# Every fourth stored o unit copied out of PSUM by VectorE instead of ScalarE

## The reference, cut to what matters

```python
# layer 0: four Gaussian kernels over adj (8, 1024, 1024)
w  = exp(-0.5 * (adj[..., None] - mean)**2 / (1e-14 + precision**2))
w  = w / sum(w, axis=-1)                     # over the four kernels
ws = sum(w, axis=2)                          # row sums, (8, 1024, 4)
x  = layernorm(x + concat_k(ws[..., k] * (x @ W_k.T)))
# layer 1: one of four experts for each batch, picked by argmax
W   = expert_w[argmax(mean_rows(x) @ router_w + router_b)]
out = adj @ (x @ W)
y   = relu(batchnorm over all rows of the same expert (out))
x   = layernorm(x + y)
```

## Time and profile before

| what | before |
|---|---|
| time, median of 3 runs | 892.62 us (890.96 to 893.26) |
| time of the profiled execution | 888.44 us |
| its span | 886.7 us |
| busy PE | 751.8 us, 85% |
| busy DVE | 754.0 us, 85% |
| busy ACT | 766.9 us, 86% |
| busy POOL | 687.5 us, 78% |

### The profile page before, as it was taken

The page is one execution under the profiler, slowest core; times in us unless marked ns, Lnnn a source line. Parts: engine busy times, 40 slices in busy tenths (PEclk is TensorE's granted clock), DMA queues, the critical chain, the costliest instruction groups (busy, mean ns, idle before and its releaser), DMA issues.

```text
span 886.7 us, 12501 instructions
## 1 busy us (share of the span) xinstructions
PE 751.8 (85%) x3922; PEld 349.1 (39%) x3922; DVE 754.0 (85%) x1639; ACT 766.9 (86%) x774; POOL 687.5 (78%) x773
## 2 busy tenths in 40 slices
PE   1444469899999999999999999999999989996671
PEld 1111124344444444444444444444444434444440
DVE  1999988899999999999999999999999981226994
ACT  5999998999999999999999999999999941116983
POOL 6699999999988888888888888888888441004794
PEclk9966679999999999999999999999999999998996
DMA  8799886898897779777977797789786636219999
GB/s 229 200 282 257 189 243 166 221 202 206 201 240 192 192 190 240 196 194 190 237 198 191 195 240 196 192 189 242 198 190 161 124 141 263 95 64 396 356 383 366
DMA packets 263925, 191.71 MB, mean 216 GB/s; under 512 B 210098, under 2 KB 210098, under 8 KB 262322
## 3 DMA queue, kind: packets, MB, share of 16 engines
q1 hardware_dynamic: 263714, 190.90, 79.3%
q10 hardware_dynamic: 144, 0.00, 0.0%
HBM read 91.78 MB, written 48.76 MB: 159 GB/s over the span
## 4 chain that ended last, share of the span: by engine, by line
ACT 38%; DVE 27%; POOL 19%; PE 9%; issue 4%; DMA 1%; SPq 0%; POOLq 0%; DVEq 0%; ACTq 0%
DVE ps_t L953 19%; ACT wgt L647 13%; ACT ps_t L656 6%; ACT ps_t L658 6%; ACT adj_in L641 5%; ACT ps_t L652 5%; PE ps_z L1118 5%; POOL adj_cut L505 3%; DVE x_in L937 3%; DVE wgt L915 3%; PE ps_o L1136 2%; POOL adj_in L500 2%; POOL x_turn L516 2%; PE ps_t L1136 2%; POOL adj_cut L503 2%
## 5 line engine op out<-in xcount | busy, mean ns | idle before, releaser
L1118 PE MATMUL ps_z<-adjT,x1p 128*128 128x512 f16 x1536 | 341.7, 379 | 0.5 <-POOL x1p L542 0.5
L953 DVE TENSOR_TENSOR ps_t<-ps_t,wgt 128x1024 f32<-128x1024 f32 x192 | 234.8, 1223 | 28.0 <-ACT ps_t L652 26.9
L1104 PE MATMUL ps_h<-w0T,x_turn 128*128 128x512 f16 x768 | 194.5, 407 | 75.1 <-DVE x_in L937 64.2
L915 DVE SCALAR_TENSOR_TENSOR wgt<-wgt,ps_t 128x1024 f32<-128x1024 f32 x192 | 224.7, 1214 | 15.8 <-ACT ps_t L658 15.8
L1118 PEld LDWEIGHTS ps_z<-adjT,x1p 128*128 128x128 f16 x1536 | 150.0, 98 | 181.3 <-POOL x1p L542 1.0
L641 ACT ACTIVATE wgt<-adj_in,neg_mu 128x1024 f32<-128x1024 f32 x192 | 205.6, 1134 | 8.4 <-POOL adj_in L500 8.2
L647 ACT ACTIVATE wgt<-wgt 128x3072 f32<-128x3072 f32 x64 | 176.5, 2758 | 0.0
L1136 PE MATMUL ps_o<-zT,w_sel 128*128 128x512 f16 x696 | 159.7, 379 | 4.8 <-DVE zT L884 3.5
L1104 PEld LDWEIGHTS ps_h<-w0T,x_turn 128*128 128x128 f16 x768 | 75.0, 103 | 184.4 <-issue 105.1
L505 POOL TENSOR_TENSOR adj_cut<-adj_in,adj_cut 128x1024 f16<-128x1024 f32 x64 | 136.6, 2134 | 5.4
L1136 PEld LDWEIGHTS ps_o<-zT,w_sel 128*128 128x128 f16 x696 | 67.9, 98 | 87.7 <-DVE zT L884 4.5
(11 more groups left out here) (220 smaller groups left out, 774.2 us busy)
## 6 DMA issues: line engine op xcount, KB each, us to landing
adj_in<-in_adj_dram SPq DMA_DIRECT2D x64, 512.0 KB, 4.1
x_in<-in_x_dram SPq DMA_DIRECT2D x64, 256.0 KB, 4.3
x_spill<-x_in SPq DMA_DIRECT2D x28, 512.0 KB, 3.4
out_spill<-o_stage SPq DMA_DIRECT2D x50, 256.0 KB, 3.1
w_sel<-w_planes SPq DMA_DIRECT2D x8, 1024.0 KB, 7.5
adjT<-x_spill SPq DMA_DIRECT2D x6, 1024.0 KB, 10.1
out_dram<-adjT SPq DMA_DIRECT2D x5, 1024.0 KB, 6.7
adjT<-out_spill SPq DMA_DIRECT2D x4, 1024.0 KB, 12.7
```

The source lines that it names most:

```text
L915: v.scalar_tensor_tensor(out=wgt[:, m % 2, j, :], in0=wgt[:, m % 2, j, :], scalar=SUM_SCALE / W0_SCALE, in1=tot, op0=ALU.mult, op1=ALU.mul ...
L953: v.tensor_tensor(tot, tot, wgt[:, n % 2, j, :], ALU.add).then_inc(dve_tot, 1)
L1104: last = te.matmul(ps_h[:, n % 2, :], xT[:, n % 2, left, c, :], w0T[:, right, c, :], start=(c + i == 0), stop=(c == C - 1 and i == 2))
L1118: last = te.matmul(ps_z[:, u % 2, :], x1p[:, b % 2, left, t, k * P:(k + 1) * P], adjT[:, b % 2, right, t, half * HALF:(half + 1) * HALF], ...
```

## The change

`take_o` is split between two engines. Units with u % 4 = 3 and u < 50 (3, 7, ... 47, twelve units) are copied by VectorE, in step n = u + 14, between `y_stats` and `low_z`. ScalarE skips them. All waits for "unit u was taken" go through a helper that picks the semaphore of the engine that takes it.

```diff
+        def taken_by_dve(u):
+            return u % G == G - 1 and u < KEPT
+
+        def taken(u):
+            if taken_by_dve(u):
+                return dve_o, u // G + 1
+            return act_o, u + 1 - min(u + 1, KEPT) // G
...
-                    sp.wait_ge(act_o, u)
+                    sp.wait_ge(*taken(u - 1))
...
             def take_o(n):
                 for u in o_units(n):
+                    if taken_by_dve(u):
+                        continue
...
+            def take_o(u):
+                dve.wait_ge(pe_o, u + 1)
+                wait(dve, o_stored[1], u // 2 * 16)
+                dve.wait_ge(dve_ostat, u)
+                v.tensor_copy(out_unit(u), ps_out(u)).then_inc(dve_o, 1)
...
-                    dve.wait_ge(act_o, u + 1)
+                    dve.wait_ge(*taken(u))
...
                 if 0 <= n - 2 < TILES:
                     y_stats(n - 2)
+                for u in o_units(n - 1):
+                    if taken_by_dve(u):
+                        take_o(u)
                 for u in z_unit(n - 1):
                     low_z(u)
...
-                wait(pe, act_o, u - 1 if u > KEPT + 3 else u)
+                ahead = u - 2 if u > KEPT + 3 else u - 1
+                if ahead >= 0:
+                    pe.wait_ge(*taken(ahead))
```

More of the change, by code:

```diff
@@ L153, in gnn_program @@
             sem(f"dve_{k}") for k in ("tot", "ws", "rest", "y", "stat", "mv"))
-        dve_z, dve_ostat, dve_omv, dve_sumT = (sem(f"dve_{k}") for k in ("z", "ostat", "omv", "sumT"))
+        dve_z, dve_o, dve_ostat, dve_omv, dve_sumT = (sem(f"dve_{k}") for k in ("z", "o", "ostat", "omv", "sumT"))
         dve_routing, dve_route = sem("dve_routing"), sem("dve_route")
@@ L602, in affine @@
                                     b_sb[:, b, C + k:C + k + 1], ALU.mult, ALU.add).then_inc(pool_affine, 1)
-            pool.wait_ge(act_o, TILES)
+            pool.wait_ge(*taken(TILES - 1))
             pool.wait_ge(dve_affine, C)
@@ L734, in affine @@
                 if n < 2:
-                    act.wait_ge(act_o, TILES)
+                    act.wait_ge(*taken(TILES - 1))
                 if n > 0:
@@ L1024, in _ @@
             assert done[0] == BN_DONE
-            dve.wait_ge(act_o, TILES - G)
+            dve.wait_ge(*taken(TILES - G - 1))
             for k in range(C):
```

## The result

The changed kernel takes 893.55 us (median of 17 runs, 891.83 to 896.78) against 890.58 us for the kernel before on the same chips (17 runs, 888.51 to 893.26). The ratio is 1.0037, 95% interval 1.0027 to 1.0048: slower by 3.3 us (2.4 to 4.3), where 4.1 us were forecast. The profiled execution took 895.25 us with a span of 893.4 us.

What follows compares the result with a forecast made beforehand. The `tot` hand-over between VectorE and ScalarE was taken as the bound. Costs of 0.7 + 3.4 = 4.1 us on the profiled 888.44 gave 892.5, plus 4.2 made 896.7 us; likeliest 895 to 899, 8 in 10 893.8 to 899.4.

Steps and rivals of the forecast that it cites:

- The bound: VectorE and ScalarE hand `tot` to and fro; the chain runs over sums and exponentials, with o and z copies beside it.
- ScalarE's relief: Twelve o copies of 0.48 us leave ScalarE, 5.8 us of work, worth 0 because Ln waits for VectorE's third sum.
- The price of the copy: VectorE's 128x512 f32 copy from PSUM to SBUF: 0.66 to 0.69 us long, pitch 0.60, between 0.33 and 0.73.
- The two slacks: VectorE's spare time per moved step: 0.34 ahead of L915 plus 0.11 before L652 at n % 8 = 1; 0.03 at n % 8 = 5.
- dense start of the row sums: In n % 8 = 1 the first L915 was to have a pitch of 1.10 instead of 1.14, gaining 0.04 us.
- The sum: Six n % 8 = 1 steps cost 0.7 us and six n % 8 = 5 steps 3.4 us, 4.1 us in all.
- What queues behind: Low plane of z, GpSimd's aggregation, SP's store and the next o product come later behind VectorE's copy; all covered, none charged.
- (a): `low_z` 0.60 later makes TensorE's o product 0.5 us late in n % 8 = 1; covered by about 0.4 and TensorE's idle time.
- Rival C: Late low plane makes TensorE the bound after n % 8 = 1: 3.0 us more, 7.1 in all, 899.7 us; chance 0.12.
- The time: Forecast median of the changed kernel: 896.7 us, 0.46% slower than 892.62.
- wide range of times: The 8 in 10 range for the changed kernel's time, 893.8 to 899.4 us.
- 4.2 us between the profiled execution and the median: Median 892.62 lay 4.2 us above the profiled 888.44; the same was added to 892.5 to forecast the changed kernel's time.

Runs made afterwards that it cites:

- u % 4 = 0: The change with VectorE copying the twelve units 4 to 48 with u % 4 = 0 in place of u % 4 = 3; ratio 1.0032 to the kernel before.
- the faster version: Kernel before with one L937 (kernel 2 of the layer 0 residual) moved ahead of the first sum in all steps; ratio 0.9957, run again 0.9959.

## Why the prediction was right

*The bound.* Right: the loop over `tot`, with the o copy of ScalarE beside it. ScalarE's relief was priced at 0 and is 0, shown from both sides (both engines copy, and neither does but for 4 columns).

*The price of the copy.* Forecast 0.69 or less long with a pitch of 0.60; measured 0.667 and 0.59.

*The two slacks.* Forecast 0.34 + 0.11 = 0.45 and 0.03 us, from the idle time ahead of the row sums, the overlap of neighbours, and the distance from the last accumulator read to the exponential. Steps came out 0.11 x 6 + 0.57 x 6 by the forecast and 0.15 x 6 + 0.57 x 6 by the trace. The 0.04 taken off for a dense start of the row sums was mis-sized: the first L932 had a pitch of 1.13 (474.11 - 472.98), not 1.10, and L661 came 0.14 late. The prediction also read the earlier trace rows too broadly where it says that VectorE waits twice in nearly every step: each wait stands there 34 times, and 500 us hold 45 or 46 steps. Step 45 has no idle time ahead of the row sums, step 44 none ahead of the first sum; that a step's slack is its own is what the experiments rest on.

*The sum.* 4.1 forecast; 4.3 in the steps; 3.3 (2.4 to 4.3) timed. The 0.34 of step 36 accounts for a part of the difference between steps and time, if it is in every execution of the kernel before, which one trace can't say; the rest is within the interval.

*What queues behind.* Covered, as forecast, but (a) was counted too high: the o product started 0.24 us later against Ln (472.44 - 470.64 = 1.80, before 468.51 - 466.95 = 1.56), not 0.5, because it followed the end of the low plane by 0.05 where I had allowed 0.3. GpSimd's wait grew from 21.4 to 26.7 us and nothing waited for it longer. Rival C was not needed: the copies that delay no o product cost the same 0.15.

*The time.* 896.7 was forecast for a kernel whose median then stood at 892.62; over 17 runs that median is 890.58. Two of the three microseconds between 896.7 and 893.55 are this, not the change. So 893.55 lies just under the 893.8 at which the wide range of times began, while the cost itself, 3.3 us, lies well inside it (1.2 to 6.8 us above 892.62). The term at fault is the 4.2 us between the profiled execution and the median, taken as the same in both kernels: by the 17 runs it is +2.1 before and -1.7 in the change. One trace and three runs could not give it, with step 14 moving single executions by more.

## What to carry to other kernels

Where two engines hand one buffer to and fro, ask what the chain goes through, not which engine is busier: work that leaves the engine beside the chain is worth nothing, and work that comes to the other costs its pitch less the slack of exactly that step. Read this slack for each kind of step, at both ends: the same copy cost 0.15 us in one and 0.57 in the other, since the second already carried four aggregations. And before moving work between engines look for an instruction inside the chain that fits a gap beside it: that gave 3.7 us where the change lost 3.3.

## What the runs showed of the hardware

- VectorE copies f32 from PSUM to SBUF at 1.05 ns a column: 138 ns for 4, 399 for 256, 667 for 512 columns; in step 41 of the change the next instruction, which does not wait for it, starts 0.08 us before its end.
- Where VectorE is the later one, ScalarE starts the instruction that waits for the accumulator read 0.09 to 0.10 us after the read's end (step 44 before, steps 41 and 45 of the change).
- TensorE's wait for one DMA of 1 MB, the first expert's weights, was 0.2 us in one trace (u % 4 = 0) and 5.1 in another (the faster version).
